# Last group of a recommendation tower: second stage with the batch rows on the partitions, the output by one VectorE instruction

## The reference

```python
for W in (W0, W1, W2):
    xk = relu(einsum('bmd,bhd,mhk->bkd', x0, xk, W))
    outs.append(sum(xk, axis=2))
h = concatenate([z, dense_ctx], axis=1)      # 1024 x 208
h = maximum(h @ W_top1 + b_top1, 0.0)        # 208 -> 512
h = maximum(h @ W_top2 + b_top2, 0.0)        # 512 -> 256
y = h @ W_top3                               # 256 -> 1
```

## Time and profile before

| | |
|---|---|
| median of 3 runs | 665.38 us (665.16 to 666.02) |
| the profiled execution: its time | 664.73 us |
| the profiled execution: its span | 662.1 us |
| PE busy | 579.3 us (88%) |
| DVE busy | 596.7 us (90%) |
| ACT busy | 357.2 us (54%) |
| POOL busy | 449.3 us (68%) |
| mean granted TensorE clock | 0.982 |

### The profile page before, as it was taken

One profiled execution on the slowest core, in us unless ns is written; L12 is line 12 of the kernel. 1 busy time (PEld: TensorE's weight loads), 2 busy tenths in 40 slices (PEclk: granted clock), 3 DMA queues, 4 the chain that ended last, 5 costly groups with the idle time before them and its releaser, 6 DMA issues.

```text
span 662.1 us, 7662 instructions
## 1 busy us (share of the span) xinstructions
PE 579.3 (88%) x2868; PEld 206.9 (31%) x2868; DVE 596.7 (90%) x332; ACT 357.2 (54%) x582; POOL 449.3 (68%) x363
## 2 busy tenths in 40 slices
PE   0046779989898989999999989999999989899996
PEld 0012223323232323333334323333334323334355
DVE  1039888999999999999999999999999999999991
ACT  0006463757546564757666465647576664644642
POOL 6676768697958878796969688787969691801010
PEclk9997979999899999999999999999999999999998
DMA  5386594728082744637280837446381908100000
GB/s 157 54 302 170 198 299 103 290 47 304 4 265 90 203 152 109 244 62 290 40 313 3 228 126 208 148 117 236 62 290 34 318 5 286 60 1 0 1 2 0
DMA packets 26990, 96.36 MB, mean 146 GB/s; under 512 B 7397, under 2 KB 12394, under 8 KB 22730
## 3 DMA queue, kind: packets, MB, share of 16 engines
q1 hardware_dynamic: 18762, 93.77, 43.0%
q0 software_dynamic: 8192, 2.11, 2.9%
HBM read 80.12 MB, written 15.73 MB: 145 GB/s over the span
## 4 chain that ended last, share of the span: by engine, by line
DVE 58%; PE 19%; issue 13%; DMA 5%; POOL 2%; ACT 1%; SPq 1%; DVEq 0%; ACTq 0%
DVE prod L415 55%; PE acca L488 6%; PE accb L488 6%; DMA rows<-field_dram 3%; PE acc L464 3%; POOL emb L326 2%; PE spread L536 1%; DVE zb_yv L419 1%; DVE za L419 1%; DMA field_dram<-zin_field 1%; PE acc L507 1%; PE accb L507 1%; SPq L256 1%; ACT zin_field L583 0%; DVE prod L400 0%
## 5 line engine op out<-in xcount | busy, mean ns | idle before, releaser
L326 POOL DMA_INDIRECT emb<-in_table,idx x256 | 246.2, 962 | 82.2 <-issue 71.6
L488 PE MATMUL accb<-prod,w 128*64 128x512 f32 x960 | 223.2, 610 | 28.4 <-DVE prod L415 28.3
L488 PE MATMUL acca<-prod,w 128*64 128x512 f32 x1024 | 231.5, 600 | 7.3 <-DVE prod L415 6.1
L339 POOL TENSOR_TENSOR prod<-rows,mates 128x1024 f32<-128x1024 f32 x70 | 163.8, 2378 | 0.8 <-issue 0.6
L415 DVE TENSOR_TENSOR prod<-rows,x1a 128x2048 f32<-128x2048 f32 x64 | 145.3, 2272 | 5.9 <-ACT x1a L588 3.8
L415 DVE TENSOR_TENSOR prod<-rows,x2b 128x2048 f32<-128x2048 f32 x64 | 145.3, 2271 | 2.1 <-PE accb L488 1.9
L415 DVE TENSOR_TENSOR prod<-rows,x2a 128x2048 f32<-128x2048 f32 x64 | 145.2, 2271 | 1.1 <-PE accb L488 1.1
L415 DVE TENSOR_TENSOR prod<-rows,x1b 128x2048 f32<-128x2048 f32 x64 | 145.2, 2270 | 0.9 <-PE accb L488 0.6
L488 PEld LDWEIGHTS accb<-prod,w 128*64 128x64 f32 x960 | 66.5, 140 | 176.1 <-issue 116.6
L488 PEld LDWEIGHTS acca<-prod,w 128*64 128x64 f32 x1024 | 73.0, 138 | 150.4 <-issue 143.3
L588 ACT ACTIVATE x1a<-acc 64x512 f32<-64x512 f32 x62 | 35.3, 570 | 126.8 <-PE acc L464 126.1
(11 more groups left out here) (56 smaller groups left out, 254.4 us busy)
## 6 DMA issues: line engine op xcount, KB each, us to landing
rows<-field_dram SPq DMA_DIRECT2D x30, 2048.0 KB, 8.9
field_dram<-zin_field SPq DMA_DIRECT2D x32, 256.0 KB
mates<-field_dram SPq DMA_DIRECT2D x16, 512.0 KB, 3.9
emb<-in_table,idx POOLq DMA_INDIRECT x256
field_dram<-zin_field SPq DMA_DIRECT2D x32, 128.0 KB
field_dram<-zin_field SPq DMA_DIRECT2D x16, 192.0 KB
rows<-field_dram SPq DMA_DIRECT2D x2, 1024.0 KB, 7.1
rows<-field_dram SPq DMA_DIRECT2D x1, 1536.0 KB, 12.7
```

The lines of the kernel that those rows point to most:

```text
L326: pool.indirect_dma_start(out=emb[q % EMBS][:, j * EMB:(j + 1) * EMB], out_offset=None, in_=table, in_offset=bass.IndirectOffsetOnAxis(ap= ...
L339: nc.gpsimd.tensor_tensor(prod0[:, (q * L0 + k) % RING0, :], rows[:, slot(q, t), :], mates[:, :], ALU.mult).then_inc(s_prod0p, 1)
L488: mm = nc.tensor.matmul(acc[j % 2][side * HID:(side + 1) * HID, :], (w1 if layer == 1 else w2)[:, step, :], prod[:, (made(layer, s, half, ...
```

## The change

For the last group alone:

- the first stage signals after each block of 128 channels (s_last1), and ACT does each relu as its block is there, with a signal after each (s_last_h1);
- the second stage is turned round: the weights of PE are now h1 (block k, 128 channels by 128 rows of the batch), the moving operand is t2 (256 columns), four matmuls that add into one 128x256 block of PSUM, acc[1], with the rows of the batch on the partitions. Its bias comes in by one more matmul, of a row of ones by the row b2, ahead of them and ahead of the wait for zb;
- relu, the product with W_top3 and the sum over the 256 channels are one DVE instruction, scalar_tensor_tensor with accum_out, into y_last, 128x1. The two relus L662, the matmuls L540 and the copy L665 are gone for this group;
- SP writes y_last to y_out: one number from each of 128 partitions;
- SP loads two more operands into the buffer mates once POOL's last layer-0 product is done: the row W_top3 repeated on 128 partitions (128 KB), and b_top2 as a row (1 KB). POOL sets 128 ones there by a memset.

```diff
--- before.py
+++ after.py
@@ -188,6 +188,9 @@
         zb, yv = zb_yv[0:HID + CTX, :], zb_yv[YV:YV + 1, :]
         h1 = sb("h1", [P, TOP1 // P, 4 * BT])
         h2 = sb("h2", [P, TOP2 // P, 4 * BT])
+
+        w3_row, b2_row = mates[:, 0:TOP2], mates[0:1, TOP2:2 * TOP2]
+        ones, y_last = mates[0:1, HALF:HALF + P], mates[:, HALF + P:HALF + P + 1]
         w0_swapped = h1[:, :, :].rearrange("p m b -> p (m b)")[:, 0:L0 * HID].rearrange("p (t k) -> p t k", k=HID)
 
         x1 = [ps(f"x1{n}", [P, HALF]) for n in "ab"]
@@ -196,6 +199,7 @@
         acc0 = ps("acc0", [P, HALF])
         spread = ps("spread", [P, HALF])
         tower = spread
+        top2_last = acc[1]
 
         field_dram = nc.dram_tensor("field_dram", [LISTS, LENGTH, N], fp32, kind="Internal").ap()
 
@@ -217,6 +221,8 @@
         s_half12, s_half3 = sem("s_half12"), sem("s_half3")
         s_za, s_zb = sem("s_za"), sem("s_zb")
         s_tower, s_act, s_y = sem("s_tower"), sem("s_act"), sem("s_y")
+        s_wide, s_ones = sem("s_wide"), sem("s_ones")
+        s_last1, s_last_h1, s_last2, s_last_y = sem("s_last1"), sem("s_last_h1"), sem("s_last2"), sem("s_last_y")
 
         def tower_cols(g):
             first, count = TOWER[g]
@@ -301,9 +307,15 @@
                 mates_in(q)
                 for g in range(len(GROUPS)):
                     rows_in(q, g)
-            for g in range(len(TOWER)):
+
+            sp.wait_ge(s_prod0p, (PERIODS - 2) * L0)
+            sp.dma_start(w3_row, bass.AP(w_top3.tensor, w_top3.offset, [[0, P], [1, TOP2]])).then_inc(s_wide, 16)
+            sp.dma_start(b2_row, b_top2.rearrange("(o n) -> o n", o=1)).then_inc(s_wide, 16)
+            for g in range(len(TOWER) - 1):
                 sp.wait_ge(s_act, stages_before(g + 1))
                 sp.dma_start(y_out[tower_cols(g), :].rearrange("b o -> o b"), yv[:, tower_cols(g)]).then_inc(s_y, 16)
+            sp.wait_ge(s_last_y, 1)
+            sp.dma_start(y_out[tower_cols(len(TOWER) - 1), :], y_last).then_inc(s_y, 16)
             sp.wait_ge(s_y, len(TOWER) * 16)
 
         @block.gpsimd
@@ -364,6 +376,8 @@
                 gather(q + 1, q)
                 for k in range(L0):
                     product0(q, k)
+            pool.wait_ge(s_prod0p, (PERIODS - 2) * L0)
+            nc.gpsimd.memset(ones, 1.0).then_inc(s_ones, 1)
             halve(PERIODS)
             halve(PERIODS + 1)
 
@@ -445,6 +459,11 @@
                         product0(1, k)
             sum3(LAST)
 
+            dve.wait_ge(s_wide, 32)
+            dve.wait_ge(s_last2, 1)
+            nc.vector.scalar_tensor_tensor(w3_row, top2_last[:, 0:TOP2], 0.0, w3_row, ALU.max, ALU.mult,
+                                           accum_out=y_last).then_inc(s_last_y, 1)
+
         @block.tensor
         def _(pe):
             def turn_fields(q, towers):
@@ -519,16 +538,9 @@
                 if stage < top1_stages(g):
                     m = [slice((parts * stage + j) * P, (parts * stage + j + 1) * P) for j in range(parts)]
                     pe.wait_ge(s_za, first + count)
-                    if last_group(g):
-
-                        pe.wait_ge(s_z2, SUBS)
-                        pe.wait_ge(s_z3, SUBS - 2)
-                        for j in range(parts):
-                            nc.tensor.matmul(top1_sums(g, j), t1a[:, m[j]], za[:, cols], start=True, stop=False)
                     pe.wait_ge(s_zb, first + count)
                     for j in range(parts):
-                        if not last_group(g):
-                            nc.tensor.matmul(top1_sums(g, j), t1a[:, m[j]], za[:, cols], start=True, stop=False)
+                        nc.tensor.matmul(top1_sums(g, j), t1a[:, m[j]], za[:, cols], start=True, stop=False)
                         mm = nc.tensor.matmul(top1_sums(g, j), t1b[:, m[j]], zb[:, cols], start=False, stop=True)
                 elif stage == top1_stages(g):
                     for j in range(TOP2 // P):
@@ -540,6 +552,33 @@
                         mm = nc.tensor.matmul(tower[0:1, 0:width], t3[:, k:k + 1], h2[:, k, 0:width],
                                               start=(k == 0), stop=(k == TOP2 // P - 1))
                 mm.then_inc(s_tower, 1)
+
+            def last_tower(g, fields):
+                first, count = TOWER[g]
+                cols = tower_cols(g)
+                m = [slice(j * P, (j + 1) * P) for j in range(TOP1 // P)]
+                pe.wait_ge(s_act, stages_before(g))
+                pe.wait_ge(s_field, fields)
+                pe.wait_ge(s_za, first + count)
+
+                pe.wait_ge(s_z2, SUBS)
+                pe.wait_ge(s_z3, SUBS - 2)
+                for j in range(TOP1 // P):
+                    nc.tensor.matmul(top1_sums(g, j), t1a[:, m[j]], za[:, cols], start=True, stop=False)
+
+                pe.wait_ge(s_z3, SUBS - 1)
+                pe.wait_ge(s_wide, 32)
+                pe.wait_ge(s_ones, 1)
+                nc.tensor.matmul(top2_last[:, 0:TOP2], ones, b2_row, start=True, stop=False)
+                pe.wait_ge(s_zb, first + count)
+                for j in range(TOP1 // P):
+                    nc.tensor.matmul(top1_sums(g, j), t1b[:, m[j]], zb[:, cols], start=False,
+                                     stop=True).then_inc(s_last1, 1)
+                for k in range(TOP1 // P):
+                    pe.wait_ge(s_last_h1, k + 1)
+                    mm = nc.tensor.matmul(top2_last[:, 0:TOP2], h1[:, k, 0:count * BT], t2[:, k, :], start=False,
+                                          stop=(k == TOP1 // P - 1))
+                mm.then_inc(s_last2, 1)
 
             pe.wait_ge(s_ident, 1)
             turn_fields(0, 0)
@@ -569,8 +608,7 @@
                         turned += 1
                     for k, q in SUM0.get((j, i), []):
                         layer0(k, q)
-            for stage in range(stages(len(TOWER) - 1)):
-                tower_step(len(TOWER) - 1, stage, turned)
+            last_tower(len(TOWER) - 1, turned)
 
         @block.scalar
         def _(act):
@@ -704,8 +742,10 @@
                         tower_step(*TOWER_AT[j, i])
             z3(SUBS - 2)
             z3(SUBS - 1)
-            for stage in range(stages(len(TOWER) - 1)):
-                tower_step(len(TOWER) - 1, stage)
+            for j in range(TOP1 // P):
+                act.wait_ge(s_last1, j + 1)
+                nc.scalar.activation(h1[:, j, 0:TOWER[-1][1] * BT], top1_sums(len(TOWER) - 1, j), ACT.Relu,
+                                     bias=b1[:, j:j + 1]).then_inc(s_last_h1, 1)
 
 
 def kernel(**inputs):
```

## The result

Median 667.52 us (664.92 to 670.22, 22 runs) against 665.06 us (661.03 to 666.02, 22 runs) before: ratio 1.0051, 95% interval 1.0038 to 1.0064, or 3.4 us slower (2.5 to 4.3). The forecast was 661.6.

A forecast was written before the change was run, and what follows sets the result against it. It took 9.2 us behind zb, at the kernel's end, as a pure series that bounds the time. Second stage 3.16 plus third stage 1.08 minus transfer 0.49 saves 3.75 us: 665.38 to 661.6, range 660.3 to 663.7.

The forecast's parts named there:

- The output transfer: Last transfer, 128 pieces of 4 bytes: 0.49 us extra, 0.18 for issue and 0.31 for landing; upper bound 1.39 plus 0.18.
- The rival "slower": Last transfer costs so much that it eats the other savings of 4.24 us; at 6 us, time 667.1; chance 0.02.
- First stage: Last group's relus start after the first block, at 653.43, so the second stage starts at 653.84 instead of 655.31.
- Second stage: Last group's eight records of 256 columns at full clock; saves 3.16 us, 1.47 from earlier start and 1.69 from clock.
- The prediction's argument that the clock stays up until a second idle stretch comes: At the end, PE's 1.40 us idle stretch alone did not lower the clock; rival of a fall anyway, 663.5, chance 0.13.
- Third stage: One DVE instruction, 0.40 us plus 0.10 for its accumulation, replaces two relus, product and copy; saves 1.08 us.
- Covered work: Bias matmul (0.46 us) falls into PE's wait for zb; earlier loads and POOL's memset are hidden too; all cost nothing.
- The sum: Whole kernel: 3.16 + 1.08 − 0.49 gives 3.75 us saved, median 665.38 to 661.6.

The follow-up runs named there:

- before_elements: Kernel before with only the last transfer changed to 128 pieces of 4 B from 128 partitions: 670.40 us, ratio 1.0069 (1.0041 to 1.0098).
- Probe 9: Ninth of twelve test transfers appended one after the other behind the end of the kernel before, 128 pieces of 4 B into SBUF: 1.74 us.
- before_again: Kernel before, unchanged, profiled once more, on the chip of 689 us: ratio 0.9984 (0.9949 to 1.0020).
- probe3: Kernel before with twelve test transfers appended, 4 B from each of varying numbers of partitions: 31 packed pieces took 4.60 us; old second stage 3.80 us, clock low.
- after_row: Changed kernel with only its last transfer put back to one row of 512 B from one partition: 661.52 us against 664.42, ratio 0.9949 (0.9927 to 0.9972).
- the turned version: Changed kernel with y turned back into a row by PE and ACT before the output: 661.67 us against 664.42, ratio 0.9955; on another chip 0.9961.

## Why the prediction was wrong, step by step

- **The output transfer: the step that failed.** I put its extra at 0.49 us, with 1.39 as upper bound (and 0.18 for the issue). It was 7.74 − 1.49 = 6.25, and 5.55 in the old end (before_elements). The issue is a small part (0.36 for 0.23). Both bounds came from rows of transfers that do something else: loads into SBUF of 4-byte pieces and loads of 128 rows of 1 KB. Probe 9 shows how little such a row says: into SBUF the same 128 pieces take 1.74 us, packed in DRAM 7. The text named the difference (those write SBUF and the new one DRAM) and bounded it by them all the same.
- **The rival "slower"** had the place, the sign and the size of the transfer, 6 us. Its chance of 0.02 was too low, and calling loads evidence against it was the error behind that. That its 667.1 lies so near the measured 667.5 is in part luck: it keeps the whole saving of 4.24 us and so is 1.8 us slower than before, where the ratio gives 3.4 (2.5 to 4.3). Its price for each of 128 pieces in a series isn't what the runs show either: 16 pieces cost next to nothing, and 128 pieces 64 B apart 0.3 us over the row. The Trainium skill's line on transfers under 512 B ("DMA: Bandwidth & Descriptors", Specifications) was the warning. The runs bear it out only in part: small pieces were dear packed side by side, and cheap spread out.
- **First stage**: relus from 0.52 us after the first matmul on zb (0.51 predicted), 0.25 to 0.27 apart, no cost of the added signals seen. PE's second stage began 0.99 after it (0.92 predicted): the first relu was ready at 654.74, but PE was on its own fourth block until 654.84, which the prediction put 0.1 us too early.
- **Second stage**: eight records, 1.94 us (1.98 predicted), clock 1.00. The working for the profiled execution was right. But 1.69 us of the 3.16 saved were the clock's, and those exist only in executions in which it fell before: three of six traces. The prediction's argument that the clock stays up until a second idle stretch comes held in its one trace only: in before_again and probe3 it fell before that. Up to the issue the new end gains 7.69 − 3.51 = 4.2 us over the kernel before as profiled (and 8.43 − 3.51 = 4.9 over before_again) and 6.1 − 3.5 = 2.6 over an old end at full clock; after_row measured 3.4 (1.9 to 4.8), in between.
- **Third stage**: one DVE instruction of 0.42 us and a separate one of 0.08 that reads the accumulator (0.40 and 0.10 predicted); it began 0.12 us after PE's end, not 0.02. The issue followed 3.51 us after the first matmul on zb, where the prediction had 656.37 − 652.92 = 3.45.
- **Covered work**: right. The bias matmul stood at 652.30, ended before zb was ready, and the loads were issued at 577.12 and 577.50, with POOL's memset (0.19 us) between its products and its next wait.
- **The sum with the measured term**: +6.25 − 2.6 to − 4.2 gives 2.1 to 3.7 us slower; measured 3.4 (2.5 to 4.3). The measured value lies near the end that has full clock before. So a second term of the sum, the 1.69 us of the clock, was probably too large for the median run, but it is the transfer that turns the gain into a loss.

## What to carry to other kernels

An operation's output layout is part of its price: a result with one number on each partition leaves as 128 pieces, and packed side by side in DRAM they took 7 us, where one row took 1.1. At the end of a kernel, nothing hides that; turning the column into a row first, on PE and ACT, cost 0.74. And what a transfer in the other direction took is no bound: without a row of the same kind, the range has to stay open on that side.

## What the runs showed of the hardware

- Packed writes of 4 B into DRAM: 8 or 16 pieces 1.1 to 1.3 us, 24 to 32 pieces 3.4 to 4.8, 48 and more 6.8 to 8.5. 128 pieces 8 or 16 B apart 3.0 to 3.1, 32 B apart 1.6, 64 B apart 1.4; 128 packed pieces of 8 B 3.0, of 16 B 1.8, of 32 B 1.4. The one other order tried cost the same (7.8), and so did one engine against sixteen (31 pieces 4.6, 32 pieces 4.8).
- The extra time lies between the last packet and the semaphore. What the memory does in it no run shows; it stays open, as does the step between 16 pieces and 24.
- The granted clock fell in the old end in three of six traces, all six with idle stretches of 1.47 and 1.23 us around the first stage; in two of the three it fell between them. It fell in none of six traces in which the second stretch was gone and, in five, the first was down to 0.85 us.
- One chip took 689 us for what the others did in 664 to 665; the ratio of the turned version to the kernel before was the same on it, 0.9961 and 0.9955.
